# A layer-norm, attention and feed-forward block on one core: first modulation split by sequence, one more head by seven products, later steps put in another order

## The chip, the cores and the metric

The kernel runs on one core of a Trainium2 chip. The metric is the device time of one execution in microseconds (us). TensorE is the matrix engine, VectorE, ScalarE and GpSimd are the other compute engines (DVE, ACT and POOL in the rows, PE for TensorE), and SyncE (SP) issues most of the DMA transfers.

## The reference, cut to what matters

`x` is 8 sequences of 128 tokens with 256 features; `cond` is 8 x 256.

```
ada = cond @ ada_w + ada_b                    # six parts: shift1, scale1, gate1, shift2, scale2, gate2
x1  = layernorm(x) * (1 + scale1) + shift1
q, k, v = split(x1 @ qkv_w + qkv_b)           # 16 heads of 128
a   = softmax(q k^T / sqrt(128)) v ;  a = a @ out_w + out_b
y   = x + gate1 * a
x2  = layernorm(y) * (1 + scale2) + shift2
x3  = y + gate2 * (gelu(x2 @ ffn_w1 + b1) @ ffn_w2 + b2)
h   = relu(x3 @ ternary(W_fc)^T) ** 2         # 1024 hidden
out = x + rmsnorm(h) @ ternary(W_proj)^T
```

## The kernel before, in words

Features lie on the partitions, tokens along the free axis. A **quad** is four sequences, 512 tokens, the free size of one PSUM bank; there are two. The 256 features are two chunks, k = 0 and k = 1. Every float32 product is taken in three fp32r products: operands are split into a rounded high part (`_hi`, made mostly by ScalarE) and the rest (`_lo`, made by VectorE or GpSimd), and hi x hi, hi x lo and lo x hi are accumulated in one bank (`split_mm`). A product of one 256-row weight block with a quad is so 2 x 3 = 6 matmuls of 512 columns.

The 16 heads are taken in four groups of four. A group has eight units: unit j is head j % 4 of quad j // 4. Most heads get query and key of both quads by a scheme with **seven block products** in place of eight (`pair_p1` to `pair_p7`, three matmuls each, 21 in all against 24): it needs sums of the weight blocks (`ws`, by GpSimd in `weight_sums`, split in `ws_hi_part` and `ws_lo_part`) and sums of x blocks (`xc`, by VectorE in `x_sums`), and between the accumulated products ScalarE copies partial results (`copy_p1`, `copy_u2`, `copy_u3`, `pair_k0`) and VectorE joins them (`pair_q0`, `pair_k1`, `pair_q1`). Group 0 takes its heads 0, 1 and 2 the plain way (`qk_products`), and head 3 by seven products.

Each engine has its own queue, written out by hand in program order; the engines meet only in semaphores. A unit on TensorE is `scores` (four fp32 products), `transpose_p` of the unit before, projections or value blocks (`v_block`), `pv` and the output product. VectorE takes the row maximum (`negmax`), ScalarE the exponentials with their row sums (`exps`), VectorE the reciprocal, GpSimd multiplies (`normalise`, semaphore `norm_done`), TensorE transposes, VectorE copies to `probT`. Groups 1 to 3 run in a hardware loop on every engine, with the end of the last group and the start of the first written out.

The start: x comes in two halves of two sequences, VectorE and GpSimd normalise it, TensorE transposes it, and `modulate(0, ...)` applies scale and shift: ScalarE the four sequences of chunk 0, VectorE those of chunk 1. `first_query` then runs the query product of head 0, `project` the key product, `first_values` the values of the first sequence. `keep_awake(n)` are products of the identity matrix with itself, whose results nobody reads. In the rows a product of two fp32 operands shows as two instructions, so `keep_awake(3)` is six. `copy_xT(0, ...)` keeps the raw x transposed, for the residual.

The end of attention: for each quad `accumulate` adds the last head group, `gate_y` multiplies by gate1 and adds the residual, `transpose_y` turns the sum back for the layer norm (`stats_of`, `normalise`). For quad 0 this is in the last units, for quad 1 in the first chunks of the first feed-forward (`ffn1`, eight chunks; Gelu by ScalarE into two buffers `hbuf`).

The last stage: `ternary1(quad, c)` is chunk c of the first ternary product (four matmuls), `ternary_r` and `ternary_r_lo` the square of relu and its low part on VectorE, `ternary2(quad, c, seqs)` the second product (two matmuls a sequence), `add_squares` and `sum_squares` the RMS norm, `finish(b)` scales sequence b and adds x. Two chunks of quad 1 are squared by ScalarE (`ON_SCALAR`). There are fewer banks than outputs: TensorE's second product for sequences 1 and 2 of quad 1 goes into banks that `finish(0)` and `finish(1)` must have read:

```
for s in seqs:
    if quad and c == 0 and s in (1, 2):
        pe.wait_ge(fin, s)
```

## Time and profile before

| | |
|---|---|
| median of 3 runs | 350.14 us (349.57 to 350.66) |
| the profiled execution | 350.69 us, of which the span from first to last instruction is 348.9 us |
| busy: TensorE / VectorE / ScalarE / GpSimd | 342.3 / 222.4 / 220.2 / 148.7 us |
| mean granted TensorE clock | 0.996 of full speed |

The page gives the busy time of each engine, the span in 40 slices, the chain of work that ended last, and the groups of instructions. The timeline lists instructions in order of time: start in us, duration in us, engine, line of the kernel, what it writes and reads, how many were merged, and in brackets how long the engine had been idle and what ended that. Matmuls overlap: the time from one start to the next is what one costs, not its duration.

### The profile page before, as it was taken

The page shows a single profiled execution, that of the slowest core. Times are in us where ns is not written, and L with a number is a line of the kernel's source. Part 1 is how long each engine was busy: PE and PEld are TensorE (multiplying, and loading weights), DVE is VectorE, ACT ScalarE, POOL GpSimd, SP SyncE. Part 2 cuts the span into 40 slices and gives each one's busy share as a digit, 9 for nine tenths or more (in the row PEclk, how much of TensorE's full clock was granted, in tenths as well). Part 3 has the DMA queues.
Part 4 walks back from the last instruction along what each step waited for, and adds up shares of the span by engine and source line. Part 5 has one row for each costly group of instructions (what it writes and reads, how often), then busy time and mean ns, then how long its engine had stood idle before and what let it go on. Part 6 is the DMA issues. An engine that isn't in the chain of part 4 may idle for free.

```text
span 348.9 us, 5879 instructions
## 1 busy us (share of the span) xinstructions
PE 342.3 (98%) x1950; PEld 293.7 (84%) x1950; DVE 222.4 (64%) x386; ACT 220.2 (63%) x560; POOL 148.7 (43%) x140
## 2 busy tenths in 40 slices
PE   8999999999999999999999999999999999999995
PEld 7888888889888888888888888888787788889884
DVE  6676756553555664456466454585875788577796
ACT  2773565667576657756664675667579536876593
POOL 3571329736534964644595573479341100000000
PEclk9999999999999999999999999999999999999998
DMA  6953003100300320030020002020000000000002
GB/s 176 362 192 120 3 0 120 62 1 3 120 0 0 120 60 0 0 120 0 25 95 0 0 6 115 0 62 0 4 0 2 0 2 0 0 2 1 1 32 90
DMA packets 12338, 16.53 MB, mean 47 GB/s; under 512 B 720, under 2 KB 8992, under 8 KB 12320
## 3 DMA queue, kind: packets, MB, share of 16 engines
q1 hardware_dynamic: 12136, 16.16, 14.2%
q8 instruction: 10, 0.16, 0.2%
q10 hardware_dynamic: 184, 0.15, 0.1%
q14 instruction: 8, 0.07, 0.1%
HBM read 15.25 MB, written 1.05 MB: 47 GB/s over the span
## 4 chain that ended last, share of the span: by engine, by line
PE 74%; issue 20%; DVE 3%; ACT 1%; POOL 1%; POOLq 0%; ACTq 0%
PE bank L1228 16%; PE bank L1230 16%; PE bank L1229 16%; PE bank L1315 8%; PE bank L1298 8%; PE bank L1304 4%; PE bank L1427 2%; PE bank L1442 1%; DVE yT L976 1%; DVE yT L966 1%; PE bank L1463 1%; PE bank L1422 1%; DVE yT L962 0%; ACT prob L579 0%; ACT hbuf L718 0%
## 5 line engine op out<-in xcount | busy, mean ns | idle before, releaser
L391 POOL TENSOR_TENSOR prob<-prob,rinv 128x512 f32<-128x512 f32 x32 | 36.2, 1131 | 60.3 <-DVE rinv L1025 59.9
L579 ACT ACTIVATE prob<-bank,negmax 128x128 f32<-128x128 f32 x128 | 45.4, 365 | 25.6 <-DVE negmax L1012 25.6
L1315 PEld LDWEIGHTS bank<-probT,vals 128*128 128x128 f32 x256 | 33.3, 191 | 3.2 <-issue 0.8
L952 DVE SCALAR_TENSOR_TENSOR o_lo<-bank,bias,o_hi 128x512 fp32r<-128x512 f32 x32 | 23.9, 745 | 17.2 <-ACT o_hi L532 17.2
L532 ACT ACTIVATE o_hi<-bank,bias 128x512 fp32r<-128x512 f32 x32 | 21.9, 686 | 19.4 <-PE bank L1315 19.4
L1315 PE MATMUL bank<-probT,vals 128*128 128x128 f32 x256 | 33.9, 275 | 0.0
L350 POOL TENSOR_TENSOR wqk_lo<-raw_qk,wqk_hi 128x512 fp32r<-128x512 f32 x16 | 21.2, 1323 | 19.6 <-ACT wqk_hi L493 18.1
L488 POOL TENSOR_TENSOR xr<-raw_qk,xt 128x256 f32<-128x256 f32 x1 | 0.7, 721 | 67.2 <-ACT raw_qk L796 67.2
L1012 DVE TENSOR_REDUCE negmax<-bank 128x4 f32<-128x512 f32 x32 | 21.8, 682 | 7.9 <-PE bank L1298 7.9
L1228 PE MATMUL bank<-wv_hi,x_hi 128*128 128x512 f32 x62 | 26.1, 420 | 0.0
L579 ACT ACTIVATION_READ_ACCUMULATOR prob<-bank,negmax 128x1 f32 x128 | 26.0, 203 | 0.0
L1025 DVE RECIPROCAL rinv<-rowsum 128x4 f32<-128x4 f32 x32 | 5.7, 177 | 31.2 <-ACT prob L579 31.2
L1228 PE MATMUL bank<-o_hi,wo_hi 128*128 128x512 f32 x64 | 25.3, 395 | 0.0
L1230 PE MATMUL bank<-o_hi,wo_lo 128*128 128x512 f32 x64 | 25.0, 390 | 0.0
L1229 PE MATMUL bank<-o_lo,wo_hi 128*128 128x512 f32 x64 | 24.9, 390 | 0.0
L1230 PE MATMUL bank<-wv_hi,x_lo 128*128 128x512 f32 x62 | 24.4, 393 | 0.0
L1229 PE MATMUL bank<-wv_lo,x_hi 128*128 128x512 f32 x62 | 24.2, 390 | 0.0
L1228 PE MATMUL bank<-x_hi,wqk_hi 128*128 128x512 f32 x54 | 24.0, 445 | 0.0
L537 ACT ACTIVATE vals<-bank 128x512 f32<-128x512 f32 x32 | 19.0, 601 | 4.5 <-PE bank L1230 3.4
L1230 PE MATMUL bank<-x_hi,wqk_lo 128*128 128x512 f32 x54 | 21.2, 393 | 0.0
L1229 PE MATMUL bank<-x_lo,wqk_hi 128*128 128x512 f32 x54 | 21.1, 392 | 0.0
L897 DVE COPY probT<-bank 128x512 f32<-128x512 f32 x29 | 19.8, 683 | 2.0 <-PE bank L1304 2.0
(218 smaller groups left out, 974.1 us busy)
## 6 DMA issues: line engine op xcount, KB each, us to landing
raw_qk<-in_L_cond_qkv_w_dram SPq DMA_DIRECT2D x6, 512.0 KB, 4.6
raw_v<-in_L_cond_qkv_w_dram SPq DMA_DIRECT2D x4, 512.0 KB, 4.1
raw_o<-in_L_cond_out_w_dram SPq DMA_DIRECT2D x4, 512.0 KB, 3.5
t_w<-in_L_cond_ada_w_dram SPq DMA_DIRECT2D x1, 1024.0 KB, 8.9
raw_w<-in_L_cond_ffn_w_dram SPq DMA_DIRECT2D x2, 512.0 KB, 6.9
t_raw<-in_L_ffn_W_fc_dram SPq DMA_DIRECT2D x4, 256.0 KB, 3.7
t_raw<-in_L_ffn_W_proj_dram SPq DMA_DIRECT2D x4, 256.0 KB, 3.8
raw_qk<-in_L_cond_ffn_w_dram SPq DMA_DIRECT2D x1, 1024.0 KB, 4.9
```

Source lines behind the costliest of these rows:

```text
L350: nc.gpsimd.tensor_tensor(lo, raw, hi.bitcast(F32), ALU.subtract).then_inc(lo_sem, 1)
L391: nc.gpsimd.tensor_tensor(e, e, rinv[:, j % 2, :].unsqueeze(2).broadcast_to([P, SQ, P]), ALU.mult).then_inc(norm_done, 1)
L532: nc.scalar.activation(hi, psum, ACT.Identity, bias=bias[:, bass.ds(at, 1)]).then_inc(hi_sem, 1)
L579: e = nc.scalar.activation(prob[:, j % 2, s, :], bank[BS][:, s * P:(s + 1) * P], ACT.Exp, bias=negmax[:, j % 2, s:s + 1], accum_out=rowsum ...
L897: nc.vector.tensor_copy(probT[:, :, :].rearrange("p s t -> p (s t)"), bank[BV][:, :]).then_inc(p_done, 1)
L952: nc.vector.scalar_tensor_tensor(out=lo[:, :], in0=bank[BO][:, :], scalar=bias[:, bass.ds(HG * G + VB + j % HG, 1)], in1=hi[:, :].bitcast( ...
L1012: nc.vector.tensor_reduce(negmax[:, j % 2, :], bank[BS][:, :].rearrange("p (s t) -> p s t", s=SQ), axis=AX.X, op=ALU.max, negate=True).the ...
L1228: nc.tensor.matmul(dst, ah, bh, start=start and n == 0, stop=False, skip_group_check=True)
L1229: nc.tensor.matmul(dst, ah, bl, start=False, stop=False, skip_group_check=True)
L1230: m = nc.tensor.matmul(dst, al, bh, start=False, stop=stop and n == len(terms) - 1, skip_group_check=True)
L1298: m = nc.tensor.matmul(bank[BS][:, t], q[:, t], k[:, t], start=True, stop=True)
L1315: m = nc.tensor.matmul(bank[BO][:, s * P:(s + 1) * P], vals[:, b, h], probT[:, s, :], start=True, stop=True)
```

## The change

In the start:
- The four bias loads are issued by ScalarE's queue, at its head, and no longer by SyncE's.
- The first modulation, `modulate_first`, is split by sequence: VectorE takes sequences 0 and 1, ScalarE 2 and 3, both first in chunk 1 and then in chunk 0. TensorE transposes chunk 1 first.
- `first_qk` takes the query and key product together, chunk 1 first; the raw transposes of chunk 1 stand between the chunks, and `keep_awake(3)` goes. Half of the copy of xT goes to VectorE, as does the low part of the weights of head 1, which was GpSimd's.
- `scores(0, 0)` goes between the last two value products; `scores(0, 1)` and `transpose_p(0, 0)` go ahead of the first modulation product of the second set.
- Head 2 of group 0 is taken by seven products, with two of the modulation products (`ada_product`) between them. GpSimd's `weight_sums` has twice the columns for it. VectorE's `x_sums` goes ahead of `unit(0, 1)`.

At the end of attention:
- `add_x` is split from `gate_y` and releases each chunk by itself; `transpose_y` goes chunk by chunk. For quad 1 accumulate, gate and add go to chunks 1, 2 and 3 of the feed-forward, and the transposes to chunk 6 instead of 5.

In the last stage:
- TensorE takes `ternary2(0, 6)` and `ternary2(0, 7)` behind `ternary1(1, 0)` and `ternary1(1, 1)`, and the sum of squares of quad 0 behind chunk 2. VectorE's list is reordered; `finish(0)` and `finish(1)` go from steps 2 and 3 to 3 and 4.

```diff
@@ SyncE, ScalarE @@
-            for src, at, n in ((qkv_b, QB, 3 * H), (out_b, OB, KD), (ffn_b1, F1B, NC), (ffn_b2, F2B, KD)):
-                sp.dma_start(brow[at - NA:at - NA + n, :], src.rearrange("(n p) -> n p", p=P)).then_inc(bias_in, 16)
+            for src, at, n in ((qkv_b, QB, 3 * H), (out_b, OB, KD), (ffn_b1, F1B, NC), (ffn_b2, F2B, KD)):
+                act.dma_start(brow[at - NA:at - NA + n, :], src.rearrange("(n p) -> n p", p=P)).then_inc(bias_in, 16)
@@ GpSimd @@
                 if j == 1:
                     if isinstance(G, int):
+                        ws_lo_part(0, 2)
                         ws_lo_part(0, 3)
...
-            wqk_lo_part(1, 2)
             rstd_of(1)
             pool.wait_ge(xn_done, 2)
             wqk_lo_part(2, 3)
             pool.wait_ge(wqk_in, 32)
-            weight_sums(0, 3, 4, 0)
+            weight_sums(0, 2, 4, 0)
@@ ScalarE @@
+            def modulate_first():
+                act.wait_ge(ada_ready, 1)
+                for k, src, full, hi in ((1, bank[7], m1_a, hi1_a), (0, bank[6], mod_a, xs_hi)):
+                    act.wait_ge(xt0_done, KD - k)
+                    for b in range(SQ // 2, SQ):
+                        m = nc.scalar.activation(xq0[:, k, b * P:(b + 1) * P], src[:, b * P:(b + 1) * P], ACT.Identity,
+                                                 bias=ada[:, SHIFT1 + k, b:b + 1], scale=ada[:, SCALE1 + k, b:b + 1])
+                    m.then_inc(full, 1)
+                    act.wait_ge(full, 1)
+                    hi_part(x_hi[:, k, SQ // 2 * P:SQ * P], xq0[:, k, SQ // 2 * P:SQ * P], hi)
...
+            ws_hi_part(0, 2)
+            o_hi_part(0, 0)
+            copy_p1(0, 2)
             ws_hi_part(0, 3)
-            o_hi_part(0, 0)
-            keep_k0(2, 5)
+            copy_u2(0, 2)
+            copy_u3(0, 2)
+            pair_k0(0, 2)
@@ VectorE @@
             ada_part(0, 0, GATE1, bank[5])
-            modulate(0, SHIFT1, SCALE1, bank[0:2])
+            modulate_first()
+            dve.wait_ge(xraw_mm, 1)
+            nc.vector.tensor_copy(xT[:, 1, cols(0)], bank[BS][:, :]).then_inc(xT1_done, 1)
             dve.wait_ge(small_cp, 4)
             keep_q0(0, 0, 1)
+            dve.wait_ge(wqk_h, 2)
+            nc.vector.tensor_tensor(wqk_lo[:, :, P:2 * P], raw_qk[:, :, P:2 * P], wqk_hi[:, :, P:2 * P].bitcast(F32),
+                                    ALU.subtract).then_inc(wqk_l, 1)
             dve.wait_ge(x1_in, 16)
             stats_of(1)
             unit(0, 0)
             modulate(1, SHIFT1, SCALE1, bank[6:8])
+            x_sums()
             unit(0, 1)
             keep_qk1(0, 0, 3, BQ, BK)
-            x_sums()
+            x_sums_lo(0)
+            x_sums_lo(1)
             keep_qk1(1, 0, 4, BE, BY)
-            x_sums_lo(0)
-            keep_q0(2, 0, 5)
-            x_sums_lo(1)
+            pair_q0(0, 2)
+            pair_k1(0, 2)
             ada_part(1, GATE1, NA, bank[7])
-            keep_qk1(2, 0, 6, BE, BY)
+            pair_q1(0, 2)
...
+            def add_x(quad):
                 dve.wait_ge(xT_done, quad + 1)
+                dve.wait_ge(xT1_done, 1)
                 for c in range(KD):
                     dve.wait_ge(gate_mul, KD * quad + c + 1)
-                    m = nc.vector.tensor_tensor(yT[:, c, cols(quad)], yT[:, c, cols(quad)], xT[:, c, cols(quad)], ALU.add)
-                m.then_inc(gated, 1)
+                    nc.vector.tensor_tensor(yT[:, c, cols(quad)], yT[:, c, cols(quad)], xT[:, c, cols(quad)], ALU.add).then_inc(gated, 1)
...
                 if c == 1:
                     accumulate(NU - 1, NG - 1, 1, last=True)
+                if c == 2:
                     gate_y(1)
-                if c == 5:
+                if c == 3:
+                    add_x(1)
+                if c == 6:
                     dve.wait_ge(gt_mm, 2)
                     stats_of(3)
...
-                if c == 1:
+                if c == 2:
                     row_scale(0)
-                if c in (2, 3):
-                    finish(c - 2)
+                if c in (3, 4):
+                    finish(c - 3)
@@ TensorE @@
-            transpose_raw(0, (bank[BE], bank[BS]))
-            keep_awake(3)
+            transpose_raw_half(0, 0, bank[BE])
+            def first_qk():
+                dsts = (bank[BQ], bank[BK])
                 pe.wait_ge(wqk_h, 1)
                 for k in (1, 0):
+                    if k:
+                        pe.wait_ge(hi1_d, 1)
+                        pe.wait_ge(hi1_a, 1)
+                    else:
+                        transpose_raw_half(0, 1, bank[BS]).then_inc(xraw_mm, 1)
+                        pe.wait_ge(hi0_d, 1)
+                        pe.wait_ge(xs_hi, 1)
+                    for w in (wqk_hi, wqk_lo):
+                        if w is wqk_lo:
+                            pe.wait_ge(wqk_l, 1)
+                        for n in range(2):
+                            nc.tensor.matmul(dsts[n][:, :], w[:, n * KD + k, 0:P], x_hi[:, k, cols(0)],
+                                             start=k == 1 and w is wqk_hi, stop=False)
...
-            scores(0, 0)
-            qk_products(1, 0, 0)
+            v_block(0, 2, V_FIRST[2])
             transpose_x(1, bank[6:8])
-            v_block(0, 1, V_FIRST[1])
-            v_block(0, 2, V_FIRST[2])
+            scores(0, 1)
+            transpose_p(0, 0)
             pe.wait_ge(mod_a, 2)
             pe.wait_ge(mod_d, 2)
             pe.wait_ge(ada2_in, 16)
             ada_product(GATE1, GATE1 + 2, ada_w2, bank[7])
             v_block(0, 3, V_FIRST[3])
             ada_product(GATE1 + 2, GATE1 + 4, ada_w2, bank[7])
-            scores(0, 1)
-            transpose_p(0, 0)
...
-            qk_products(2, 0, 0)
+            pair_p1(0, 2)
+            pair_p2(0, 2)
+            pair_p6(0, 2)
+            ada_product(GATE1 + 4, GATE1 + 6, ada_w2, bank[7])
+            pair_p7(0, 2)
+            pair_p5(0, 2)
             ada_product(GATE1 + 6, GATE1 + 8, ada_w2, bank[7])
-            qk_products(2, 0, 1, (BE, BY))
+            pair_p4(0, 2)
+            pair_p3(0, 2)
...
-            for c in range(NC):
+            LAG = 3
+            for c in range(NC - 2):
                 ternary2(0, c, range(SQ))
             pe.wait_ge(xs_lo, 6 * KD)
             for c in range(NC):
                 ternary1(1, c)
-                if c == 0:
+                if c < 2:
+                    ternary2(0, NC - 2 + c, range(SQ))
+                if c == 2:
                     sum_squares(0)
```

## Rows read from the trace of the kernel before

**Rows 1.** The page: busy us of the engines; TensorE's granted clock in 40 slices.
```profile
PE 342.3 (98%) x1950; PEld 293.7 (84%) x1950; DVE 222.4 (64%) x386; ACT 220.2 (63%) x560; POOL 148.7 (43%) x140
...
PEclk9999999999999999999999999999999999999998
```

**Rows 2.** What TensorE waited for: us in total, times, longest.
```profile
PE bank L1541 <- DVE yT L966: 0.4, 1, 0.4
```

**Rows 3.** Timeline of TensorE to 16 us: start, us, line, operation [idle before].
```profile
4.38 3.35 PE L1427 MATMUL bank<-ident 128*128 128x128 f32 x14
7.52 2.22 PE L1442 MATMUL bank<-condT,hbuf 128*128 128x8 f32 x16
...
11.38 0.83 PE L1427 MATMUL bank<-ident 128*128 128x128 f32 x6
12.32 0.73 PE L1480 MATMUL bank<-x_hi,wqk_hi 128*128 128x512 f32 x2
...
13.99 0.27 PE L1502 MATMUL bank<-ident,t_up 60*128 60x60 f32 x1
...
15.66 0.39 PE L1494 MATMUL bank<-wv_hi,x_hi 128*128 128x512 f32 x1
15.89 0.39 PE L1494 MATMUL bank<-wv_hi,x_lo 128*128 128x512 f32 x1
```

**Rows 4.** Timeline of ScalarE to 12 us.
```profile
4.37 0.18 ACT L667 ACTIVATE condT<-bank 128x16 f32<-128x16 f32 x1 [1.36 <-PE bank L1433]
...
10.34 1.50 ACT L520 ACTIVATE xq<-bank,ada 128x128 f32<-128x128 f32 x4 [2.10 <-PE bank L1456]
11.87 0.63 ACT L493 ACTIVATE x_hi<-xq 128x512 fp32r<-128x512 f32 x1
```

**Rows 5.** Timeline of VectorE to 16 us.
```profile
10.34 1.37 DVE L868 TENSOR_SCALAR xq<-bank,ada 128x128 f32<-128x128 f32 x4 [0.30 <-PE bank L1456]
11.74 0.43 DVE L875 CAST x_hi<-xq 128x512 fp32r<-128x512 f32 x1
...
15.40 1.39 DVE L814 BATCH_NORM_STATS2 stats<-xt 128x6 f32<-128x256 f32 x4
```

**Rows 6.** Timeline of TensorE, 24 to 29 us.
```profile
24.27 0.95 PE L1442 MATMUL bank<-condT,t_w 128*128 128x8 f32 x8
...
28.31 0.60 PE L1304 MATMUL bank<-ident,prob 128*128 128x128 f32 x4
```

**Rows 7.** Timeline of GpSimd, 20 to 25 us.
```profile
20.30 1.28 POOL L350 TENSOR_TENSOR wqk_lo<-raw_qk,wqk_hi 128x512 fp32r<-128x512 f32 x1 [1.56 <-DVE xn L833]
...
23.34 1.04 POOL L391 TENSOR_TENSOR prob<-prob,rinv 128x512 f32<-128x512 f32 x1
```

**Rows 8.** GpSimd's groups by shape: busy us, mean ns of one, idle before.
```profile
L408 POOL TENSOR_TENSOR ws<-raw_qk 128x384 f32<-128x384 f32 x3 | 3.1, 1019 | 0.0
...
L408 POOL TENSOR_TENSOR ws<-raw_qk 128x128 f32<-128x128 f32 x4 | 1.8, 461 | 0.0
```

**Rows 9.** Timeline of VectorE, 254 to 257 us.
```profile
254.76 1.89 DVE L833 TENSOR_SCALAR raw_qk<-bank,mv,rstd 128x256 f32<-128x256 f32 x4
```

**Rows 10.** Timeline of TensorE, 256 to 258 us.
```profile
256.71 1.09 PE L1463 MATMUL bank<-ident,raw_qk 128*128 128x128 f32 x8
```

**Rows 11.** Timeline of VectorE, 267 to 272 us.
```profile
267.37 1.41 DVE L976 SCALAR_TENSOR_TENSOR yT<-bank,bias,yT 128x512 f32<-128x512 f32 x2
...
270.02 1.29 DVE L966 TENSOR_TENSOR yT<-yT,xr 128x512 f32<-128x512 f32 x2
```

**Rows 12.** Timeline of TensorE, 271 to 273 us.
```profile
271.02 0.39 PE L1230 MATMUL bank<-x_hi,w_lo 128*128 128x512 f32 x1
...
272.74 0.50 PE L1228 MATMUL bank<-x_hi,w_hi 128*128 128x512 f32 x1 [0.22 <-ACT hbuf L718]
```

**Rows 13.** Timeline of VectorE, 335 to 336 us.
```profile
335.05 0.48 DVE L1177 SCALAR_TENSOR_TENSOR xr<-bank,rms,xt 128x256 f32<-128x256 f32 x1
```

**Rows 14.** Timeline of TensorE, 335 to 336 us.
```profile
335.58 0.39 PE L1656 MATMUL bank<-wqk_lo,hid_hi 128*128 128x256 f32 x1
```

More of the change, by code:

```diff
@@ L686, in _ @@
             wqk_hi_part(3, 32)
+            keep_v(1, 2, V_FIRST[1])
+            keep_v(2, 3, V_FIRST[2])
             modulate(1, SHIFT1, SCALE1, bank[6:8])
-            for b in range(1, SQ):
-                keep_v(b, b + 1, V_FIRST[b])
+            keep_v(3, 4, V_FIRST[3])
             act.wait_ge(max_done, 2)
@@ L763, in square_relu, with ternary_hidden @@
                 nc.scalar.activation(hbuf[:, n % 2, :], relu[:, n % 2, :], ACT.Square).then_inc(r_done, 1)
-            def ternary_hidden(quad, c, between=None):
+            def ternary_hidden(quad, c):
                 n = NC * quad + c
@@ L782, in _ @@
                     relu_of(0, c + 1)
-                ternary_hidden(0, c, between=(lambda: x3_hi(1)) if c == NC - 1 else None)
+                if c == NC - 1:
+                    x3_hi(1)
+                ternary_hidden(0, c)
             relu_of(1, 0)
@@ L1420, in transpose_raw @@
                         pe.wait_ge(x0_in[s // 2], 16)
-                    for k in range(KD):
-                        m = nc.tensor.transpose(dst[k][:, s * P:(s + 1) * P], xt[:, quad * SQ + s, k * P:(k + 1) * P], ident[:, :])
+                    m = nc.tensor.transpose(dst[:, s * P:(s + 1) * P], xt[:, quad * SQ + s, k * P:(k + 1) * P], ident[:, :])
+                return m
+            def transpose_raw(quad, dst):
+                for k in range(KD):
+                    m = transpose_raw_half(quad, k, dst[k])
                 m.then_inc(xraw_mm, 1)
@@ L1537, in transpose_y @@
             def transpose_y(quad):
-                pe.wait_ge(gated, quad + 1)
-                for s in range(SQ):
-                    for c in range(KD):
+                for c in range(KD):
+                    pe.wait_ge(gated, KD * quad + c + 1)
+                    for s in range(SQ):
                         m = nc.tensor.transpose(bank[BACK[quad][s // 2]][:, (s % 2) * D + c * P:(s % 2) * D + (c + 1) * P],
```

166 lines of the change are left out of this document (80 added, 86 removed).

## The prediction

> **What bounds the kernel now.** I read the page's busy table first: TensorE is busy 98% of the span and its granted clock is full nearly everywhere [rows 1]. A busy TensorE says little, since its matmuls overlap, so I looked next at the waits of TensorE. Nothing there is long: the longest after the start is 0.4 us, at the first transpose back of the gated sum [rows 2]. The chain that ended last is TensorE almost throughout. So the bound is TensorE's own list in its order, and the change is worth (a) matmuls taken off this list, (b) starting it sooner, (c) waits it takes away, less (d) waits it adds. In the timeline one fp32r product of 512 columns takes its turn every 0.23 us (15.66 to 15.89) [rows 3], eight fp32 transposes or small products 0.80 us plus about 0.09 us at the change of kind. The other engines matter where TensorE asks for a result sooner than they have it. I laid the four engines' queues out in program order, with these durations, for the three stretches that the change touches.
>
> **Part 1, the loads moved from SP to ACT.** Four small bias loads leave SP and stand on ACT ahead of its table load. ACT makes condT at 4.37 us [rows 4], and TensorE first uses it at 7.52, behind its keep-awake products [rows 3]: 3.1 us of cover, where ACT makes nothing else that is waited for. On SP everything behind them (values, rest of the query and key weights, second half of x, the modulation weights) is issued sooner; nobody in the stretch after 12 us waits for a load, so that gives nothing either. Cost 0. Without the cover the condT delay would go straight into the path.
>
> **Part 2, the first modulation.** Now VectorE makes four pieces of the second half of the features (1.37 us) and a rounding copy (0.43), ScalarE four of the first half (1.50) and its copy (0.63), both from 10.34, and the first query product runs at 12.32 [rows 3 to 5]. Afterwards each engine does two sequences of k=1 first. VectorE: 2 x 0.34, half a copy, about 0.25: done 11.3. ScalarE: 2 x 0.375 and about 0.41 (0.63 less a fixed part): done 11.55. The first product goes at about 11.7, 0.6 us sooner. k=0 is ready at 12.6 as before. Between them TensorE has four products (0.91) and the second four raw transposes (0.45), which were idle-time work before, so they now count. k=0, four products, ends at 14.0; bias transpose 0.29; four products with the low parts 0.91 + switch: the values start at about 15.3 instead of 15.66. Gain 0.35 us. Bounds: today 12.32 to 15.66 is 3.34 us, of which twelve products and the bias transpose are 3.0, so 0.3 us is hand-over; with as much of it again the gain is 0.1, without any 0.55.
>
> The three keep-awake products (six rows, 0.83 us at 11.38 [rows 3]) go. They filled a wait, so this is 0; but TensorE now idles about 0.65 us before 11.7. The trace has an idle of 0.4 us further on [rows 2] with the granted clock full on both sides [rows 1], so I cost it at nothing. The Trainium skill, TensorE: Matmul & The Clock Gate, section Part 4: PE-mode transpose, says that transposes are not counted as busy by the clock gate as products are; by it the padding that goes was the work that counted between 9.7 and 12.3, and the clock could fall to 1.2 GHz. By the row the sum gets 0 here, by the rule what rival 4 works out; no run here shows such a fall.
>
> **Part 3, the order behind it, and a new wait.** TensorE's list is now: values 5 products (15.3 to 16.45), scores(0,0) 0.89, the last values product 0.23, query and key of head 1 12 x 0.227 = 2.73 (20.3), two value blocks 2.73 (23.0), transposes of x 0.80, scores(0,1) 0.80: at 24.65 it comes to the transposes of the first probabilities. Before they ran at 28.31, behind modulation products like that of 24.27 [rows 6], and GpSimd's normalisation had ended at 24.38 [rows 7]: 3.9 us of slack. Now GpSimd:
> VectorE must first copy one half of xT (0.68), bias the query, which needs the query product (about 15.1), and make wqk_lo of head 1 (0.69); so its statistics of the second half start at 16.4 and not 15.40 [rows 5]. These feed rstd (GpSimd) and the normalised x, behind which GpSimd's wqk_lo of head 2 stands: about 20.95 instead of 20.30 [rows 7], +0.65. Then the four weight sums have 256 columns and not 128. Mean of one: 461 ns at 128, 1019 ns at 384 [rows 8]; between them 740 ns, a turn every 0.70 instead of 0.42: +1.0 with rounding. The normalisation so ends at 24.38 + 1.65 = 26.05. TensorE waits from 24.65 to 26.1: **+1.45 us**. Behind it queue everything on TensorE: the modulation products, value block 3, second-half query and key. Bounds: 0.65 if the sums' size cost nothing (a turn is mostly fixed), 2.5 if GpSimd is held up by VectorE's work for another microsecond. I take 1.45, since two sizes of the very operation bracket it.
>
> **Part 4, head 2 of group 0 by seven products.** 24 products become 21: -3 x 0.227 = -0.68. Two hand-overs come in without their cover of the loop: p6 needs ScalarE's copy of p1 (0.17 + 0.60) over p2 (0.68), +0.15; and kT comes 0.17 + 0.69 after p4, over p3 alone (0.68), where in the loop other products stand between, +0.24. p7 and p4 are covered by modulation products (0.89 each), low parts of the sums by value and key products. VectorE's x sums now stand ahead of its row maximum, but the probabilities they feed are used 10 us later. Net -0.3 (bounds -0.68 and 0).
>
> The loops are untouched and TensorE has no wait there: the shift is handed on, one for one.
>
> **Part 5, the end of attention.** The residual add now releases its halves singly, and the transposes back go half by half: the first half is ready 0.6 us sooner, so the 0.4 us wait [rows 2] goes. But it is not kept. VectorE and ScalarE run a chain of their own from that add through the row maximum, exponentials, statistics to the normalisation at 254.76, 1.89 us, and TensorE's transposes of x at 256.71 start as it ends [rows 9, 10]. None of this chain waits for the transposes back, so TensorE waits 0.4 us there instead. Gain 0 (0.4 if the chain had slack I don't see).
>
> **Part 6, the first half of the feed-forward.** Today VectorE does accumulate (1.41), gate and add (1.29 each) in one block from 267.37 to 271.3 [rows 11], the low part of the hidden chunk stands behind it, Gelu behind that, and TensorE pays: the product of 271.02 is over at 271.25, the transposes start at 271.46, and after their 0.80 the next chunk could start at 272.26 but starts at 272.74 [rows 12]. Spread over chunks 1, 2, 3 each low part is late by at most 1.3 us, and each Gelu is there before TensorE's next chunk (1.37 us a chunk, two buffers); the transposes go to chunk 6, beside other transposes, which saves a switch. -0.21 - 0.48 and -0.09 for the switch: **-0.75 us** with rounding (bounds -0.85, 0). Downstream, the statistics move 0.1 us ahead of today's, TensorE 0.75; by the same laying out the normalised x is there 0.7 us before its transposes.
>
> **Part 7, the last stage.** TensorE's chunks 6 and 7 of the first product go between the chunks of the next. This removes a wait of about 0.2 us for the sum of squares and lets ScalarE run ahead. But finish(0), finish(1) move one chunk later, to VectorE's steps 3 and 4, and TensorE's product into the bank of sequence 2 waits for finish(1). Before: finish(1) at 335.05, 0.48 long, and TensorE goes at 335.58 [rows 13, 14]. After: TensorE has chunk 3 done at 330.7 and gets the root at 331.0; three half chunks of the second product (4 x 0.12 each), chunks 4 and 5 (0.91 each) and one sequence (0.24) later it asks for finish(1): 334.5. Chunk 4 was out at 332.6, ScalarE has a square before it and rectifies it by 333.6, and VectorE's square, low part and sum take a turn of 0.60 each (two such in 1.29 us, 0.69 for one [rows 11]), then finish: 333.6 + 1.8 + 0.48 = 335.9. So about 1.4 us of new wait eats what was won: TensorE is at 335.9 against 335.58, and has 0.4 us fewer waits from there to the end. Net -0.1 (bounds -0.4, +0.3).
>
> **Sum.** -0.35 + 1.45 - 0.3 + 0 - 0.75 - 0.1 = -0.05 us. Against the profiled execution, 350.69 us (span 348.9 and 1.8 around it), that is 350.6. This run was 0.55 above the median of the three, 350.14; on the median it is **350.1 us: no change that can be measured**. One can tell about 0.3% from no change here, 1.05 us.
>
> **Rivals.**
> 1. The new wait does not arise, because statistics and sums are done sooner than I lay out or the sums cost little more. For it: GpSimd loses a 1.3 us job (wqk_lo of head 1). Against: that job ended before the statistics were there. -1.2 to -1.45: 348.8. Chance 0.13.
> 2. The gains at the end are kept: the 0.4 of part 5, and 0.6 in part 7 if finish(1) comes earlier: 349.0. Against: both chains stand in the trace. Chance 0.08.
> 3. Slower: the wait at the first probabilities is long. GpSimd's queue shares its time with VectorE's modulation and low parts; if normalisation and sums take 1.2 us more, it ends at 27.3 and the sum is +1.2: 351.3. It decides from 27.15 on. Chance 0.13.
> 4. Slower: the clock falls to its lower level at 11 us. For it: at the start TensorE ran at half its later rate, 14 identity products in 3.35 us against 6 in 0.83 [rows 3], and it was at work for at least 3 us before that changed. Against: the granted clock is full there. With 3 us of work at half rate, +3: 353. The rule named in part 2 is its mechanism. Chance 0.03.
> The forecast has 0.63. The range reaches from rival 1 to rival 3 with a little for the spread of the runs (349.57 to 350.66): 348.7 to 351.5. Faster: 0.13 and part of 0.08, 0.19; slower 0.16; within 0.3%, 0.65.
>
> **What would show it.** The transposes of the first probabilities start near 26.1 with an idle of about 1.4 us released by GpSimd's normalisation; the first query product near 11.7; the four sums at about 740 ns; the transposes back without a wait but the transposes of the normalised x with one of 0.4; no gap at the chunk after the second transposes back; a wait of 1 to 1.6 us on the VectorE finish near 335. It would be wrong above all if TensorE does not wait for GpSimd at 24.6, or if the clock row shows less than full after 11 us.

## The result, and the profile after

The changed kernel takes 352.85 us in the median of nine executions (351.19 to 355.08), the kernel before beside it 350.26 (349.48 to 350.80): 1.0084 times as long, with a 95% interval of 1.0063 to 1.0106. It is slower, and outside the forecast range. The first thing to see is the spread: 3.9 us against 1.3. The executions from the shortest to the longest, with the mean clock granted to TensorE (1.000 is full speed):

| us | 351.19 | 351.57 | 351.68 | 352.72 | 352.85 | 352.91 | 354.52 | 354.87 | 355.08 |
|---|---|---|---|---|---|---|---|---|---|
| clock | 0.996 | 1.000 | 0.996 | 0.995 | 0.991 | 0.995 | 0.989 | 0.990 | 0.989 |

The execution profiled is the second of these, at full clock throughout, so this profile can explain 1.3 us of the loss and not the rest of the 2.6. The page:

```profile
PE 339.3 (97%) x1941; PEld 291.5 (83%) x1941; DVE 224.3 (64%) x389; ACT 223.1 (64%) x564; POOL 149.5 (43%) x140
```

Against [rows 1], TensorE has nine instructions and 3.0 us of busy time less, in a span 0.9 us longer. What TensorE waited for (total, times, longest; waits of 0.2 us left out), where [rows 2] had 0.4 us as the longest after the start:

```profile
PE bank L1337 <- POOL prob L390: 1.6, 1, 1.6
PE bank L1464 <- POOL ident L344: 1.5, 1, 1.5
PE bank L1526 <- ACT x_hi L492: 1.4, 1, 1.4
PE bank L1704 <- DVE xr L1208: 1.3, 1, 1.3
PE bank L1331 <- ACT kT L547: 0.3, 1, 0.3
PE bank L1261 <- DVE w_lo L965: 0.3, 1, 0.3
```

The second, for the identity, is at the start of both kernels. The timeline of TensorE at the places that answer to [rows 3, 6, 10, 12, 14]:

```profile
4.37 2.34 PE L1464 MATMUL bank<-ident 128*128 128x128 f32 x14
...
8.40 1.07 PE L1493 MATMUL bank<-ident,prob 128*128 128x128 f32 x8
9.31 0.60 PE L1454 MATMUL bank<-ident,xt 128*128 128x128 f32 x4
11.34 0.70 PE L1526 MATMUL bank<-x_hi,wqk_hi 128*128 128x512 f32 x2 [1.43 <-ACT x_hi L492]
...
23.67 1.06 PE L1331 MATMUL bank<-kT,qT 128*128 128x128 f32 x8
26.29 0.66 PE L1337 MATMUL bank<-ident,prob 128*128 128x128 f32 x4 [1.56 <-POOL prob L390]
...
37.48 0.39 PE L1263 MATMUL bank<-x_hi,wqk_lo 128*128 128x512 f32 x1
38.16 0.47 PE L1261 MATMUL bank<-w_hi 128*128 128x512 f32 x1 [0.29 <-DVE w_lo L965]
...
44.10 1.15 PE L1331 MATMUL bank<-kT,qT 128*128 128x128 f32 x8 [0.35 <-ACT kT L547]
...
258.50 1.09 PE L1499 MATMUL bank<-ident,raw_qk 128*128 128x128 f32 x8
...
274.38 1.03 PE L1590 MATMUL bank<-ident,yT 128*128 128x128 f32 x8
275.25 1.06 PE L1630 MATMUL bank<-ident_bf,t_w 128*128 128x128 bf16 x16
...
336.93 0.39 PE L1704 MATMUL bank<-wqk_lo,hid_hi 128*128 128x256 f32 x1 [1.28 <-DVE xr L1208]
```

The waits of 1.56 us at 26.29 and of 1.28 us at 336.93 stand where the prediction put them. A trap is in the first row: fourteen identity products take 2.34 us here and 3.35 in [rows 3], since TensorE left its half rate a microsecond sooner. Over all profiles of this study the transposes of the first normalised x start anywhere from 8.39 to 9.63 us (the kernel before and its variants from 9.25, 9.5 in the mean of six; the changed one and its variants up to 9.47, 8.9 in the mean of fourteen). So I count from that point: to the scores of unit 2, before takes 32.8 us (9.60 to 42.38), an execution of the changed stretch at full clock 34.9 (8.39 to 43.31, the run with earlier finishes below). This one takes 35.7 (8.40 to 44.10), as its first weights landed late (ScalarE's rounding copy at 9.42 us; where they land in time the first product comes 0.8 sooner). Counting so leaves out the earlier start itself. Whether the change has a part in it is open: the loads that it moved are not the reason, since with them back on SP the transposes started at 8.86 and 8.96. GpSimd ahead of the wait, answering to [rows 7, 8]:

```profile
21.07 1.29 POOL L349 TENSOR_TENSOR wqk_lo<-raw_qk,wqk_hi 128x512 fp32r<-128x512 f32 x1 [1.55 <-DVE xn L846]
22.32 0.74 POOL L407 TENSOR_TENSOR ws<-raw_qk 128x256 f32<-128x256 f32 x1
...
24.51 0.72 POOL L412 TENSOR_TENSOR ws<-raw_qk,ws 128x256 f32<-128x256 f32 x1
25.19 1.04 POOL L390 TENSOR_TENSOR prob<-prob,rinv 128x512 f32<-128x512 f32 x1
```

### The profile page after: what moved, and what is told of

The parts are those of the page before. It is cut to its first block, busy times and chain, and to the rows that moved or that the text cites. A ratio compares the mean times of both kernels' runs of the same rounds, so it can differ in the third digit from the quotient of the medians.

```text
span 349.8 us, 5872 instructions
## 1 busy us (share of the span) xinstructions
PE 339.3 (97%) x1941; PEld 291.5 (83%) x1941; DVE 224.3 (64%) x389; ACT 223.1 (64%) x564; POOL 149.5 (43%) x140
## 4 chain that ended last, share of the span: by engine, by line
PE 64%; issue 20%; DVE 6%; ACT 5%; DMA 2%; POOL 0%; SPq 0%; POOLq 0%; ACTq 0%; DVEq 0%
PE bank L1261 15%; PE bank L1263 14%; PE bank L1262 14%; PE bank L1348 8%; PE bank L1331 7%; PE bank L1337 3%; DMA raw_qk<-in_L_cond_qkv_w_dram 1%; ACT prob L584 1%; DMA xt<-in_x_dram 1%; DVE w_lo L965 1%; DVE hid_lo L912 1%; DVE yT L988 1%; ACT hbuf L731 1%; DVE x_lo L901 1%; DVE o_lo L971 1%
## 5 line engine op out<-in xcount | busy, mean ns | idle before, releaser
L349 POOL TENSOR_TENSOR wqk_lo<-raw_qk,wqk_hi 128x512 fp32r<-128x512 f32 x15 | 19.9, 1326 | 21.2 <-ACT wqk_hi L492 19.7
L1337 PE MATMUL bank<-ident,prob 128*128 128x128 f32 x128 | 19.4, 274 | 1.7 <-POOL prob L390 1.6
L1261 PE MATMUL bank<-x_hi,wqk_hi 128*128 128x512 f32 x46 | 20.5, 446 | 0.0
L912 DVE TENSOR_TENSOR hid_lo<-hbuf,hid_hi 128x512 fp32r<-128x512 f32 x24 | 16.4, 688 | 6.1 <-ACT hid_hi L492 5.9
```

Of the source, the lines that this page charges most:

```text
L349: nc.gpsimd.tensor_tensor(lo, raw, hi.bitcast(F32), ALU.subtract).then_inc(lo_sem, 1)
L1261: nc.tensor.matmul(dst, ah, bh, start=start and n == 0, stop=False, skip_group_check=True)
L1337: m = nc.tensor.transpose(bank[BV][:, s * P:(s + 1) * P], prob[:, j % 2, s, :], ident[:, :])
```

## The experiments

Every run is beside the kernel before on the same chip (medians 349.94 to 350.34); the bracket is the interval of the ratio. "Fell" counts executions with a mean clock of 0.995 or less; none of before is under 0.996.

### What makes the spread

**The same kernel again.** No edit. 

> The changed kernel once more, unchanged. Theory A: its executions differ by what clock TensorE is granted. The nine so far lie between 351.19 and 355.08 us, those above 354 with a mean granted clock of 0.989 or 0.990 and spans of 352.7 to 353.3, those below 352 with 0.996 to 1.000 and spans of 349.4 to 349.8. Then this run spreads the same way, its median is 352 to 353.5, and a profile that falls in the upper part shows one stretch with a clock below full and the same order of everything else. Theory B: the spread comes from when the first loads land, and has nothing to do with the clock; then spans and mean clocks of the executions are not in one order.


354.95 us (354.74 to 355.87), 1.0137 [1.0122, 1.0152]; fell 4 of 4. Its profile is what was missing. The page's clock in 40 slices, the windows from 25 us on (PE busy in the second column, the granted clock third from the end), and two products:

```profile
PEclk9995899999999999999999999999999999999998
```

```profile
25.00:26.00 1.00, 0.00 (x0) 0.00 (x0) 0.23 (x1) 0.97 (x3) 1.00 (x2) 1.00 0.00 0
26.00:27.00 1.00, 0.89 (x9) 0.89 (x9) 1.00 (x2) 0.18 (x1) 1.00 (x2) 1.00 0.00 0
27.00:28.00 1.00, 1.00 (x7) 1.00 (x7) 1.00 (x1) 0.00 (x0) 0.73 (x1) 0.52 0.03 8
...
30.00:36.00 6.00, 6.00 (x19) 5.01 (x18) 2.90 (x6) 4.51 (x12) 1.60 (x2) 0.50 0.40 146
...
37.00:38.00 1.00, 1.00 (x9) 0.92 (x8) 0.50 (x1) 0.00 (x0) 0.00 (x0) 0.86 0.00 0
```

```profile
33.05 0.63 PE L1263 MATMUL bank<-x_hi,wqk_lo 128*128 128x512 f32 x1
33.47 0.63 PE L1261 MATMUL bank<-x_hi,wqk_hi 128*128 128x512 f32 x1
```

TensorE is idle in the whole window 25 to 26 and works again from 26.1. From 27.0 to 37.3 the clock is at its lower level, 1.2 GHz: half of full. A product of 512 columns comes every 0.43 us and not every 0.23. That is 5 us of clock lost. Theory A holds.

**The padding at the start.** `+ keep_awake(3)` ahead of `first_qk()`. 

> The changed kernel with the three identity products put back behind the raw transposes of the first half, ahead of the wait for the first key/query weights. Theory A (the padding that went lets the clock fall in some executions): the upper executions go, the median falls from 352.9 to about 351.5 and the spread to that of the kernel before, 1.3 us. Rival: the padding is nothing, the three products run in a wait of 1.43 us (0.8 us of work at most), and median and spread stay as in the run beside it, 352 to 353.5, spread 3 to 4 us.


353.45 (351.78 to 355.51), 1.0105 [1.0071, 1.0139]; fell 4 of 6. In its profile the padding runs at 9.95 us, the first product at 10.75 has no idle time ahead of it, and the clock is down from about 26.7 to 30.1 us all the same. Neither the padding that went nor the idle time at 11 us is the cause.

**Working through the wait.**
```
 scores(0, 1)
+keep_awake(12)
 transpose_p(0, 0)
```


> The changed kernel with twelve identity products (0.114 us each, 1.4 us) between the scores of the second unit and the transposes of the first probabilities, so that TensorE works through its wait for GpSimd instead of standing idle. The wait itself stays. Theory A: the idle of 1.6 us (with hand-over 2.6 from the last product's start to the next) is what the fall of the clock to half follows, 1 to 2 us later, in some executions. Then no execution falls: median 351.2 to 351.9, spread under 1.5 us, all windows at full clock. Rival (the clock falls whatever TensorE does at 24 us, for instance because of the idle at 9.7 to 11.3 us or the fp32 transposes): median 353 to 355 and spread 3 to 4 us as in the changed kernel.


351.80 (351.43 to 352.59), 1.0056 [1.0039, 1.0073]; fell 0 of 6, spread 1.2 us. The padding, then GpSimd's normalisation beside it:

```profile
23.95 2.85 PE L1464 MATMUL bank<-ident 128*128 128x128 f32 x24
26.63 0.60 PE L1337 MATMUL bank<-ident,prob 128*128 128x128 f32 x4
```

```profile
24.60 1.04 POOL L390 TENSOR_TENSOR prob<-prob,rinv 128x512 f32<-128x512 f32 x1
```

The twelve products take 2.7 us and not the 1.4 that I had written, for each is two instructions of 0.11 us. So TensorE is held up about 1 us longer than GpSimd, which ends at 25.64, would hold it; only the idleness is gone. So the idle time at 24 to 26 us is what the falls follow.

**Scores and transposes back behind the second modulation product.** 

> The changed kernel with the scores of the second unit and the transposes of the first probabilities moved back behind the modulation products and value block 3, as before. My theory: the wait of 1.56 us of TensorE for GpSimd's normalisation at the transposes goes, since 3 us of products stand ahead of it, and the whole 1.4 us is kept to the end: 1.2 to 1.5 us faster than the run of the changed kernel beside it. If TensorE's idle time there is also what lowers the clock, up to 2.5 us and a smaller spread. Rival: the wait is not on the path that sets the end, because TensorE then waits for the weight sums, the scores or the low parts of the second modulation instead: 0 to 0.4 us.


354.39 (351.90 to 357.18), 1.0094 [1.0068, 1.0121]; fell 5 of 6. The rival was right: TensorE waited for ScalarE's modulation instead, and the clock fell behind that, from 26.8 to 33.6 us.

```profile
25.18 1.06 PE L1479 MATMUL bank<-condT,t_w 128*128 128x8 f32 x8 [1.59 <-ACT xfull L514]
```

**The whole order of before, 17 to 28 us** (transposes of the second half of x ahead of value blocks 1 and 2 too, ScalarE's second modulation ahead of its copies). 

> The changed kernel with TensorE's list between 17 and 28 us in the order of before (transposes of the second half of x straight behind the products of head 1; scores of the second unit and transposes of the first probabilities behind the second modulation product), and ScalarE's second modulation ahead of its copies of the value blocks, as before. When only scores and transposes were moved back, TensorE waited 1.59 us for ScalarE's modulation instead, since the transposes of x still came two value blocks late. My theory: now there is neither wait, TensorE has no idle over 0.4 us after 12 us, and the clock stays full: 349.0 to 350.0, spread as before. Rival: VectorE's later statistics (it has two more jobs ahead of them) make the transposes of x wait by up to 1 us, and part of the idle stays: 350.3 to 352 with falls of the clock in some executions.


351.21 (350.55 to 351.46, nine), 1.0030 [1.0018, 1.0042]; fell 0 of 9. The falls are gone, but not as cheaply as I wrote: TensorE waits 0.84 us for VectorE's normalised x, 0.58 for the sums' low part and 0.50 for the key.

**A shorter idle.** Head 2 plain, sums of 256 and then of 128 columns, the change's order otherwise (`weight_sums(0, 2, 4, 0)` and `(0, 3, 4, 0)`).


> The changed kernel with the products of head 2 of the first group as 24 plain products, as before; GpSimd still makes the sums of weights over 256 columns and VectorE its sums of x where the change put them. The idle at the first probabilities stays, and with it the falls of the clock. By the profiles head 2 by seven products took 0.5 us longer from the query of head 0, second half, to the scores of unit 2 (14.22 against 13.72 us), where I forecast 0.3 less. My theory: the profiled span is 0.3 to 0.7 us shorter than 349.8 where the clock stays full. Rival: the seven products gain their 0.68 and the loss lies elsewhere; then it is 0.3 to 0.7 us longer.


353.41 (350.50 to 355.73), 1.0083 [1.0051, 1.0116]; fell 7 of 10; wait 1.73 us.


> The changed kernel with head 2 of the first group plain and the sums of weights over 128 columns, in TensorE's order of the change. The same with sums of 256 columns waited 1.73 us at the transposes of the first probabilities, and the clock fell in 7 of 10 executions (353.4). I put the four sums at 740 against 461 ns each. Theory: the wait falls by 1.0 to 1.1 us, to about 0.6 to 0.7, and with so short an idle the clock falls in no execution: 349.8 to 350.6. Rival: the normalisation ends where it did for another reason (VectorE's statistics) and wait and falls stay: 352 to 354.


349.89 (349.12 to 350.45), 0.9995 [0.9986, 1.0004]; fell 0 of 12. Its wait, from the timeline:

```profile
25.80 0.66 PE L1331 MATMUL bank<-ident,prob 128*128 128x128 f32 x4 [0.62 <-POOL prob L390]
```

The size of the sums is worth 1.1 us of wait, and with 0.62 us of idle nothing falls.

**What stands around the idle.** The same idle in the kernel before, with two value blocks straight behind it: 

> The kernel before with the scores of the second unit and the transposes of the first probabilities moved ahead of value blocks 1 and 2; nothing else is changed. TensorE then comes to these transposes at about 22.3 us and GpSimd's normalisation ends at 24.4: an idle of 2.1 us. Theory A (such an idle is enough): 2 us of wait, and a fall of the clock in part of the executions on top: median 352 to 356, spread over 2.5 us, and windows at half clock some 1 to 2 us behind the idle. Rival: the clock needs something else of the changed kernel; then 351.8 to 352.4 with the spread of before, 1.3 us.


351.95 (351.52 to 352.53), 1.0056 [1.0040, 1.0071]; fell 0 of 6, although TensorE waited as long:

```profile
24.36 0.66 PE L1304 MATMUL bank<-ident,prob 128*128 128x128 f32 x4 [1.57 <-POOL prob L391]
```

The wait costs its length with the hand-over, 1.9 us, and nothing more. In the changed kernel, value block 3 ahead of the modulation product: 

> The changed kernel with value block 3 (six products of 512 columns) ahead of the first of the second modulation products (eight of 8 columns), not behind it. The idle of 1.6 us ahead of the transposes of the first probabilities stays. Theory C (idle alone is not enough: the clock falls when light work, transposes and products of 8 columns, stands on both sides of the idle; the kernel before with an idle of 1.57 us and twelve full products straight behind never fell in six executions): falls become fewer, median 351 to 352.5. Rival: any idle of this length in this place can be followed by a fall, and the six executions were chance: median and spread as in the changed kernel, 352.5 to 355, spread 3 to 4 us.


351.56 (350.90 to 351.84), 1.0039 [1.0024, 1.0054]; one of six at 0.995, 0.1 us above the next. And in the kernel before with the modulation product behind the idle: 

> The kernel before with the same idle as in my earlier run on it (scores and transposes of the first probabilities straight behind the transposes of x), but with a modulation product behind the transposes and the value blocks after it. Theory C (light work around the idle): falls of the clock to half in part of the executions, windows at 0.50 between 24 and 35 us, median 352 to 355.5, spread over 2.5 us. Rival (the fall needs something that only the changed kernel has, for instance its shorter dense stretch since the start or a second idle at 10 us): no fall, 351.5 to 353 by the wait alone, spread 1.3 us.


352.22 (351.61 to 354.26), 1.0067 [1.0043, 1.0092]; fell 1 of 6, to 0.991, 2 us above the rest. TensorE behind the wait in the last two, first the changed kernel with the block ahead:

```profile
26.34 0.66 PE L1337 MATMUL bank<-ident,prob 128*128 128x128 f32 x4 [1.73 <-POOL prob L390]
26.75 0.47 PE L1261 MATMUL bank<-wv_hi,x_hi 128*128 128x512 f32 x1
```

and the kernel before with the light product behind:

```profile
24.05 0.66 PE L1304 MATMUL bank<-ident,prob 128*128 128x128 f32 x4 [1.57 <-POOL prob L391]
24.55 0.96 PE L1442 MATMUL bank<-condT,t_w 128*128 128x8 f32 x8
```

Full products behind the idle all but end the falls: 10 of 13 in the changed kernel, 1 of 6 with the block ahead, and that one cost next to nothing; six executions are few. That light work alone brings them is hardly borne out: 1 of 6 in the kernel before. Theory C explains one side.

### What makes the rest

**Head 2 plain in the order of before**, sums of 128 columns. 

> The changed kernel with TensorE's order of before from 17 to 28 us (as in the run that did this alone, 351.21) and with head 2 of the first group as 24 plain products and the sums of weights over 128 columns. In that run TensorE waited 0.58 us for the low part of the sums of x and 0.50 us for the key, and the profile of before is 0.5 to 0.8 us shorter in this stretch although it has three products more. Theory: head 2 by seven products costs more than it gives where nothing stands between them: 0.5 to 0.8 us faster than 351.21. Rival: the waits would have come anyway, for other results of the late VectorE, and the three products more cost 0.68: 351.3 to 351.9.


350.00 (349.70 to 350.41), 0.9995 [0.9985, 1.0005], against 1.0030 with seven products and wide sums: 1.2 us. Both waits for the sums and the key are gone. **The added job back on GpSimd** (`wqk_lo_part(1, 2)`): 

> The changed kernel with the order of before between 17 and 28 us, head 2 plain and sums of 128 columns (350.00), and wqk_lo of head 1 back on GpSimd. In the profile of 350.00 TensorE waits 0.81 us at 21.04 for the normalised second half of x from VectorE, whose statistics stand behind that 0.69 us job. Theory: the wait falls to 0.1 to 0.3 and 0.5 to 0.7 us are kept: 349.3 to 349.5. Rival: on GpSimd the job ends later than on VectorE and TensorE waits for it at the products of head 1, or the gain is lost at the transposes of the probabilities: 349.8 to 350.2.


349.37 (348.89 to 350.04), 0.9978 [0.9967, 0.9988]. The wait for the normalised x goes from 0.81 to 0.23 us:

```profile
20.33 1.09 PE L1490 MATMUL bank<-ident,xn 128*128 128x128 f32 x8 [0.23 <-DVE xn L841]
```

**Bias loads back on SP** in the order of before. 

> The changed kernel with TensorE's order of before from 17 to 28 us and the four small bias loads back on SP's queue behind the first key/query weights. In the profiles with these loads on ScalarE's queue the rounding copy of the first weights starts at 7.70, 8.16, 8.19, 9.24 and 9.42 us, released by their load; in the kernel before at 7.61. Theory: the loads on the second queue take part of the bandwidth when the first weights land, and cost up to 1 us where they come late: 0.2 to 0.5 us faster than 351.21 on the median, and the copy starts at 7.6 to 7.8. Rival: the landing varies by itself and nothing changes, 351.0 to 351.4.


350.75 (350.24 to 351.74), 1.0021 [1.0007, 1.0035] against 1.0030: the intervals overlap, so the time does not settle it. The profiles say more: see part 1 below.

**The end.** Before, with parts 5 and 6 alone; with 5, 6 and 7; and with the first two finishes one chunk earlier as well, ScalarE's square root with them (the edit is against the changed kernel):
```
-if c == 2: row_scale(0)
-if c in (3, 4): finish(c - 3)
+if c == 1: row_scale(0)
+if c in (2, 3): finish(c - 2)
```


> The kernel before with the residual add released by halves (part 5) and gate and add of the second half spread over the feed-forward chunks (part 6), and nothing of the last stage. Theory: this is the 0.75 us of part 6, 349.3 to 349.6, and the last stage of the change (part 7) holds the other 0.3 to 0.6 of the 1.3 us that the end alone gained. Rival: part 6 gives all of it (348.9 to 349.1) and part 7 nothing.


349.20 (348.61 to 349.93), 0.9972 [0.9961, 0.9983].


> The kernel before with the end of the change alone: the residual add released by halves (part 5), the gate and add of the second half spread over the feed-forward chunks (part 6), and the last stage as the change has it (part 7). Everything up to the loop is as before. Theory: the loss is all ahead of the loop. From the scores of unit 2 to the end of the span the profile of before takes 306.5 us (42.38 to 348.9) and three profiles of the changed kernel without a fall 305.7; so this is 0.8 us faster than before, 349.2, with the spread of before and no fall of the clock. Rival: the end gains nothing by itself (the 0.8 only makes up for the later arrival): 350.0.


349.05 (348.71 to 349.73), 0.9970 [0.9959, 0.9981].


> The same with the square root, row scale and the first two finishes one chunk earlier, as before. In the changed kernel this took a further 1.0 us off the stretch from the scores of unit 2 to the end (43.31 to 348.0 is 304.7, against 305.7), all of the wait on the finish of sequence 1. Theory: 1.8 us faster than before, 348.2. Rival: that gain came with that execution, and it is 349.2 as without it.


348.21 (347.67 to 348.77), 0.9944 [0.9927, 0.9960]. From the scores of the last group's unit at 244.87 us to the last sum of squares at 343.33 the kernel before takes 98.5 us, the three take 97.6, 97.5 and 96.6. In the last, VectorE has the finish of sequence 1 at 333.11 us, 88.3 behind those scores; in the changed kernel (336.39) it was 89.7:

```profile
332.50 0.69 DVE L1189 TENSOR_TENSOR raw_qk<-raw_qk 128x512 f32<-128x512 f32 x1
333.11 0.48 DVE L1182 SCALAR_TENSOR_TENSOR xr<-bank,rms,xt 128x256 f32<-128x256 f32 x1
```

On the changed kernel itself this was the first try of it: 

> The changed kernel with ScalarE's square root of the first half after chunk 0, VectorE's row scale at its step 1 and the first two finishes at steps 2 and 3, as before. My theory: the sum of squares is now a product group later than the root is asked for, so the root stands in ScalarE's queue ahead of the next rectification; TensorE's wait of 1.28 us on the finish of sequence 1 at 336.9 falls to 0.2 to 0.6, but about 0.6 us of it returns as waits for the hidden chunks: 0.2 to 0.5 us faster. Rival: the whole 1.0 us is gained. Other rival: the earlier root stalls ScalarE and with it the chunks, and it is up to 0.5 us slower.


352.93 (349.80 to 353.97), 1.0081 [1.0053, 1.0109], fell 4 of 6; its profile, at full clock, is 1.0 us shorter from the scores of unit 2 to the end (304.7 against 305.7).

**All together**: 

> The changed kernel with the order of before between 17 and 28 us, head 2 plain with sums of 128 columns, wqk_lo of head 1 on GpSimd (349.37), and besides the first two finishes one chunk earlier and the bias loads back on SP. Left of the change are the first modulation by sequence and the end. Theory: 0.85 to 1.0 us less for the finishes and 0 to 0.3 for the loads: 348.1 to 348.5, the same as the start of before with that end (348.21), since the first modulation by sequence gains at the first product and gives it back in the wait for the normalised second half. Rival: the new start is worth its 0.35 us once its side effects are gone: 347.7 to 347.9.


348.34 (348.12 to 349.10), 0.9952 [0.9935, 0.9969]. It cannot be told from the start of before with the good end, 0.9944. Either beats the kernel before by about 2 us; the start of before with the good end needs no new start.

## Why the prediction was wrong, point by point

**Part 1, the moved loads, 0.** Too low, by some 0.2 us as an estimate. I looked only at condT on ScalarE and at loads after 12 us; what moved is the landing of the first query and key weights. ScalarE's copy of them starts at 7.70 to 9.56 us in the twelve profiles with the bias loads on its queue (8.7 in the mean), and at 7.61 to 8.21 in the eight with them on SP (7.8), whatever else was changed. In six of the twelve the first product comes 0.1 to 0.8 us later for it than its usual 2.14 us behind the fixed point (the start of the transposes of the first normalised x), 0.2 in the mean of all twelve. In the profiled execution, at 9.42, the copy itself holds up ScalarE's modulation, and it is 0.8; in the other five GpSimd's low part of these weights comes to stand beside VectorE's rounding copy of x, which takes 0.62 to 0.93 us there and 0.29 where they are apart. The medians with the loads back differ by 0.3 us and their intervals overlap, so the timed runs neither show nor exclude it.

**Part 2, -0.35.** Where the weights land in time, the first product comes 0.58 us sooner from the fixed point (2.14 us behind it against 2.72), forecast 0.6; the values start 0.22 sooner. The step was right and a little large. The keep-awake products were rightly at 0, and the Trainium skill's rule on transposes in TensorE: Matmul & The Clock Gate, Part 4: PE-mode transpose, which I had weighed there, found no support at 11 us: with the padding back the clock fell in 4 of 6 executions, without it in 10 of 13, and in both behind the later idle.

**Part 3, +1.45.** The mechanism and the size were right: 1.56 us, GpSimd's sums at 740, 730, 720 and 720 ns, VectorE's statistics at 16.33 (forecast 16.4). That the times of day agree is luck: counted from the fixed point, TensorE came to the transposes 1.3 us and GpSimd to its end 1.4 us later than I had laid out, and TensorE's earlier start made up 1.2 of it. The wait is their difference, and that was right. The two contributions came out apart as 1.1 us (sums) and 0.6 (VectorE's job, in the other order). **What failed is the price of the wait.** I put it at its own length. With the hand-over around it such a wait costs about 0.3 to 0.4 us more (1.9 for 1.57 in the kernel before). The larger miss is the clock. Part 2 had taken from an idle of 0.4 us that idleness leaves the clock alone, and rival 4 looked for a fall only at 11 us, with a chance of 0.03. The idle that I had myself worked out at 24.65 to 26.1 us was never held against the clock. So what came is rival 4's mechanism in another place, for it had 353 us. It brought a fall in 10 of 13 executions, 1.2 to 4.4 us more than the three that kept the clock; the four profiles of this study that hold a fall have 3.4 to 10.3 us at 1.2 GHz. That is about 1.3 us in the first median and 3.4 in the second.

**Part 4, -0.3.** Wrong in sign. From the query of head 0 for the second half to the scores of unit 2 take 14.22 us with seven products (29.88 to 44.10) and 13.72 with plain ones (before): this part loses 0.5 us, and in the order of before 1.2, wide sums included. The 0.68 of work is saved. The wait for kT was there (idle 0.35, and 0.5 with the hand-over, forecast 0.24). At p6 I had 0.15 for ScalarE's copy of p1, and where that decides it is 0.16 (the same kernel again); but in the first profile the low part of the x sums comes later still (idle 0.29 and 0.45 with the hand-over; 0.58 idle in the order of before), which I had called covered: its two pieces take 3.45 us on VectorE and not 2.6, next to GpSimd's own low part. Some 0.2 us more went into changes between small and large operations that I had not counted.

**Part 5, 0.** The number is as forecast, the place is not. The transposes back have no wait at 249.79, and of the 0.4 us next to nothing is left at 258.50: there TensorE is 1.79 us later than [rows 10], at the scores before the first transposes back 1.84 (246.71 against 244.87). But the transposes of the normalised x have no wait either. The time goes 2.4 us ahead of them, at the output product that needs VectorE's low part, where from the transposes of the probabilities on 0.78 us pass and not 0.36:

```profile
256.09 0.50 PE L1261 MATMUL bank<-o_hi,wo_hi 128*128 128x512 f32 x1 [0.18 <-DVE o_lo L971]
```

**Part 6, -0.75.** Right: no gap around 274.38, and with part 5 it measures -0.84 by the profiles, 0.28% (1.0 us) in the timed runs.

**Part 7, -0.1.** Right by the profiles, -0.15 (the timed runs, 0.9970 and 0.9972, can't tell it from nothing), and the new wait on the finish is 1.28 us where I had 1.4. Rival 2's remark that an earlier finish keeps 0.6 us was low: it keeps 0.9.

**The sum.** At full clock and counted from the fixed point: +2.1 us ahead of the loop where I had +0.8, +0.1 in it, -1.0 behind it where I had -0.85; together +1.2. The executions at 0.996 to 1.000 are 0.9 to 1.4 over before (351.2 to 351.7), with their earlier start and their late weights in that. Rivals 1 and 3 did not come: the wait was neither absent nor longer. So the mis-sized terms ahead of the loop are 1.3 us (0.8 in part 4, some 0.4 in the wait with its hand-over, 0.1 in part 2), and the unpriced fall of the clock is the rest.

**What stays open.** Why an idle of 1.57 us in the kernel before brings one fall in twelve executions and one of 1.56 to 1.76 in the changed kernel ten in thirteen. What stands behind it matters there; it is not the whole cause. The idle time at 11 us, which only the changed kernel has, is not it: with the padding back it is gone, and the clock falls. The dense work ahead of it, and where in time it lies (22.5 to 24 us against 24.5 to 26), were not varied by themselves.

## What to carry to other kernels

A forecast idle of TensorE has two prices: its length, and the chance that the clock falls to half behind it for several microseconds. Here an idle of 1.6 to 1.8 us in a dense stretch brought that in most executions of the changed kernel and in few of the kernel before, one of 0.6 or 0.8 us in none. Such an idle is worth filling with padding, or worth full products straight behind it. When a median moves more than the profile, look at the spread and the mean clock of all executions before looking for a cause in the one that was profiled. And compare two starts from a common operation, not from time zero.

## What the runs showed of the hardware

The half-rate period at the start ends at different times in executions of one program: fourteen identity products took 2.34 and 2.85 us in two of the changed kernel. Over all profiles they took 2.15 to 3.36. The granted clock reads full there in the windows from 4 to 8 us of the kernel before; the half rate is seen in the durations alone.

VectorE's subtraction of two operands in memory slows down beside GpSimd's. In the changed kernel two of 128x1024 took 3.45 us, and GpSimd has its own beside the second:

```profile
34.61 3.45 DVE L965 TENSOR_TENSOR w_lo<-xc,w_hi 128x1024 fp32r<-128x1024 f32 x2
```

```profile
35.68 1.30 POOL L349 TENSOR_TENSOR w_lo<-ws,w_hi 128x512 fp32r<-128x512 f32 x1 [1.16 <-ACT w_hi L492]
```

The first of the two takes 1.21 us and the second, which starts beside GpSimd's, 2.32. In the other profile of the same kernel the fall of the clock had moved them apart, and both take 1.22:

```profile
38.17 2.35 DVE L965 TENSOR_TENSOR w_lo<-xc,w_hi 128x1024 fp32r<-128x1024 f32 x2
```

```profile
35.44 1.27 POOL L349 TENSOR_TENSOR w_lo<-ws,w_hi 128x512 fp32r<-128x512 f32 x1 [1.16 <-ACT w_hi L492]
```

In the kernel before, where VectorE's started first (36.23, and GpSimd's at 36.91), VectorE's took its 1.22 us and GpSimd's 1.69 in place of 1.3. The Trainium skill, GPSIMD Engine Reference, 8. Key points, says that the two engines share their way to that memory where VectorE has two such inputs; the case fits it. No run was made to take the overlap away by itself; the profiles above are the only ones of one kernel with and without it.
